# A graph network on one core: in the last pass the own rows are added by products and the sums copied by ScalarE; in the first attention the own rows are weighted by VectorE

## The reference, cut to what matters

```python
e = a_src[src] + a_dst[dst]                 # per edge and head, then leaky relu
e_exp = jnp.exp(e - segment_max(e, dst)[dst])
alpha = e_exp / segment_sum(e_exp, dst)[dst]
out = segment_sum(h[src] * alpha[:, :, None], dst).reshape(N, 256) + bias
out = relu(out)
out = out / maximum(sqrt(sum(out * out, -1)), 1e-12)
x = layernorm(x + out)
```

## Time and profile before

| | us |
|---|---|
| median of three runs | 6150.03 |
| lowest, highest | 6143.17, 6152.39 |
| the profiled execution | 6138.69 |
| its span, first to last instruction | 6136.9 |

### The profile page before, as it was taken

How to read it: one execution, slowest core, us unless ns; L and a number is a source line. 1 busy time by engine, 2 the same in 40 slices (tenths; PEclk the granted TensorE clock), 3 DMA queues, 4 the chain that set the end, 5 groups by cost and what they waited for, 6 DMA issues and landing times. The chain is left out here.

```text
span 6136.9 us, 94789 instructions
## 1 busy us (share of the span) xinstructions
PE 5167.8 (84%) x23690; PEld 3888.2 (63%) x23690; DVE 4560.9 (74%) x13038; ACT 3817.9 (62%) x11901; POOL 3041.7 (50%) x2581
## 2 busy tenths in 40 slices
PE   2788899999999988888888998988899989945654
PEld 1566666666677776767666666667777767733443
DVE  7676655555677787887787888878878777768886
ACT  0587765666899766666655555565555567755555
POOL 1677777422444455555355665543333230057776
PEclk7899999999999999999988888889999989955555
DMA  1577543343566554545344444434544431134442
GB/s 49 183 266 255 193 136 113 125 142 112 195 221 220 184 183 165 190 171 183 137 141 155 157 154 159 161 109 141 166 153 152 137 109 54 39 115 138 139 138 94
DMA packets 362734, 925.74 MB, mean 151 GB/s; under 512 B 66872, under 2 KB 140715, under 8 KB 362198
## 3 DMA queue, kind: packets, MB, share of 16 engines
q1 hardware_dynamic: 271078, 702.73, 33.4%
q0 software_dynamic: 91120, 216.96, 12.1%
HBM read 568.39 MB, written 361.72 MB: 152 GB/s over the span
## 5 line engine op out<-in xcount | busy, mean ns | idle before, releaser
L2207 POOL DMA_INDIRECT got<-hop,end_i x600 | 642.6, 1071 | 725.0 <-PE psum L1014 466.0
L2207 POOL DMA_INDIRECT got<-tab,end_i x600 | 702.8, 1171 | 441.7 <-PE psum L1122 266.7
L1122 PE MATMUL psum<-got,sf 128*128 128x264 f32 (+2 forms) x1200 | 470.4, 482 | 365.0 <-DVE got L1946 288.4
L1014 PE MATMUL psum<-got,sf 128*128 128x256 f32 x1600 | 507.1, 399 | 104.8 <-ACT got L1278 96.8
L1122 PEld LDWEIGHTS psum<-got,sf 128*128 128x128 f32 x1200 | 238.8, 240 | 470.6 <-DVE got L1946 350.4
L1014 PEld LDWEIGHTS psum<-got,sf 128*128 128x128 f32 x1600 | 289.5, 195 | 269.4 <-issue 99.8
L2298 POOL DMA_INDIRECT out<-res,out_i x200 | 211.4, 1057 | 463.9 <-DMA out<-hd 358.0
L963 PE MATMUL psum<-h_t,w 128*128 128x512 f32 x784 | 380.3, 616 | 68.5 <-DVE h_t L1705 68.5
L1162 ACT ACTIVATE squares<-res,l_sv 128x256 f32<-128x256 f32 x600 | 297.3, 496 | 223.7 <-DVE l_sv L1851 188.7
L1278 ACT COPY got<-psum 1x256 f32<-1x256 f32 x796 | 280.0, 352 | 239.2 <-PE psum L1014 184.2
L1316 ACT ACTIVATE res<-res,l_mo 128x256 f32<-128x256 f32 x600 | 310.8, 589 | 147.7 <-DVE l_mo L1839 147.5
(11 more groups left out here) (438 smaller groups left out, 14914.2 us busy)
## 6 DMA issues: line engine op xcount, KB each, us to landing
own<-hop SPq DMA_DIRECT2D x150, 512.0 KB
x_t<-res SPq DMA_DIRECT2D x150, 512.0 KB
xo<-x_t SPq DMA_DIRECT2D x150, 512.0 KB, 3.7
hop<-res SPq DMA_DIRECT2D x100, 512.0 KB
x_in<-in_x SPq DMA_DIRECT2D x98, 512.0 KB, 4.6
out<-hd SPq DMA_DIRECT2D x98, 512.0 KB
tab<-tab SPq DMA_DIRECT2D x50, 536.0 KB, 2.7
own<-tab SPq DMA_DIRECT2D x50, 536.0 KB
```

The source lines that it names most:

```text
L1014: T.matmul(o, sf_of(q)[:, k * P:(k + 1) * P], got_of(q)[:, k * FEAT:(k + 1) * FEAT], start=(p < 3), stop=True).then_inc(at("l_agg"), 1)
L1122: T.matmul(bank(3 + k % 2)[:, 0:g.ext], sf_[:, k * P:(k + 1) * P], got_of(q)[:, k * g.width:k * g.width + g.ext], start=True, stop=True).t ...
L2207: eng.indirect_dma_start(out=dst, out_offset=None, in_=table, in_offset=bass.IndirectOffsetOnAxis(ap=idx, axis=0), bounds_check=rows_ - 1, ...
```

## The change

In the planner: pass 4's `mine` moves from GpSimd to DVE, and the lengths of `vals`, `mine`, `merge`, `u`, `sqr` and `agg` are changed; pass 6 gets ACT parts `ev0` to `ev3` and loses `rlu`. On PE, `agg` k of pass 6 becomes two products into one bank, `ident0` by the own rows and the selection matrix by the linked rows; both stand behind the wait for `g_v`. From k = 2 on they also wait for ACT's copy out of that bank. On DVE, `agg` k of pass 6 keeps only the carry row. On ACT, `ev` k waits for the DVE read of that bank and copies it with relu onto the own rows (the relu of the sum is the same before the division, whose divisor is positive). `merge` waits for the four copies. The sum per row for the shift, before an output of `rlu`, is now an accumulator output of `u`, after which DVE waits for it and scales it.

```diff
--- before.py
+++ after.py
@@ -408,22 +408,27 @@
                 put(("T", "spr", q), 1.8 if p == HOPS else 1.0, here("Vmax", "Sselm"), bank="ring", emptied=here("Vspr"))
                 put(("V", "spr", q), 0.75, here("Tspr", "Vmax") + early("S", "exp"))
                 put(("S", "exp", q), 0.3, here("Vspr") + early("V", "merge"))
-                put(("V", "vals", q), 2.0 if p == HOPS else 0.8, here("Sexp", "Ggather"))
-                me = "Gmine" if p == HOPS else "Vmine"
-                put((me[0], "mine", q), 3.1 if p == HOPS else 0.75, here("Sexp", "Yown"))
+                put(("V", "vals", q), {4: 1.45, 5: 0.8, 6: 1.45}[p], here("Sexp", "Ggather"))
+                put(("V", "mine", q), {4: 1.45, 5: 0.75, 6: 1.3}[p], here("Sexp", "Yown"))
                 put(("V", "lead", q), 0.45, here("Vvals") + early("V", "agg3", 1))
                 for k in range(K):
                     bank_ = [("V", f"agg{k - 2}", q)] if k >= 2 else [("V", f"agg{k + 2}", q - 1)] if j else [("V", "x1a0", q - 1), ("V", "x1a1", q - 1)]
-                    put(("T", f"agg{k}", q), 0.6, here("Vlead" if k == 0 else f"Vagg{k - 1}", "Ssel") + bank_)
-                    put(("V", f"agg{k}", q), 0.78 if p != 5 else 0.5, here(f"Tagg{k}", me))
+                    if p == 6:
+                        if j > 2 * ng or k >= 2:
+                            bank_ = [("S", f"ev{k - 2}", q) if k >= 2 else ("S", f"ev{k + 2}", q - 1)]
+                        put(("T", f"agg{k}", q), 1.05, here("Vlead" if k == 0 else f"Vagg{k - 1}", "Ssel", "Vmine") + bank_)
+                        put(("V", f"agg{k}", q), 0.45, here(f"Tagg{k}"))
+                        put(("S", f"ev{k}", q), 0.42, here(f"Vagg{k}"))
+                    else:
+                        put(("T", f"agg{k}", q), 0.6, here("Vlead" if k == 0 else f"Vagg{k - 1}", "Ssel") + bank_)
+                        put(("V", f"agg{k}", q), 0.78 if p != 5 else 0.5, here(f"Tagg{k}", "Vmine"))
                 free_ = room if p != 5 else ([("T", "tz", q - 2)] if i >= 2 else [])
-                put(("V", "merge", q), {4: 3.2, 5: 1.0, 6: 1.7}[p], here("Vagg3") + ([("S", "sqv", q - 2)] if p == 4 else []) + free_ + (here("Yxo") if p == 4 else []) + early("V", "merge", 1))
+                put(("V", "merge", q), {4: 2.7, 5: 1.0, 6: 1.7}[p], here("Vagg3") + (here("Sev3") if p == 6 else []) + ([("S", "sqv", q - 2)] if p == 4 else []) + free_ + (here("Yxo") if p == 4 else []) + early("V", "merge", 1))
             if p == 6:
-                put(("S", "rlu", q), 1.75, here("Vmerge") + [("V", "u", q - 2)] * (i >= 2))
-                put(("S", "sqr", q), 1.75, here("Srlu") + [("V", "sn", q - 2)] * (i >= 2))
+                put(("S", "sqr", q), 2.4, here("Vmerge") + [("V", "sn", q - 2)] * (i >= 2))
                 put(("V", "sn", q), 0.2, here("Ssqr") + [("V", "u", q - 2)] * (i >= 2))
                 put(("G", "rn", q), 1.05, here("Vsn"))
-                put(("V", "u", q), 1.8, here("Grn", "Yxo") + [("S", "sqv", q - 2)] * (i >= 2))
+                put(("V", "u", q), 2.3, here("Grn", "Yxo") + [("S", "sqv", q - 2)] * (i >= 2))
                 put(("S", "sqv", q), 2.1, here("Vu") + [("V", "sv", q - 2)] * (i >= 2))
                 put(("V", "sv", q), 0.2, here("Ssqv") + [("V", "sh", q - 2)] * (i >= 2))
                 put(("G", "rs", q), 1.05, here("Vsv") + [("S", "norm", q - 2)] * (i >= 2))
@@ -1115,12 +1120,18 @@
             elif name[:3] == "agg":
                 k = h
                 eng.wait_ge(at("g_v"), K * j + k + 1)
-                if K * j + k >= 2:
+                if K * j + k >= 2 * ng * K + 2:
+                    eng.wait_ge(at("g_ev"), K * i + k - 1)
+                elif K * j + k >= 2:
                     eng.wait_ge(at("g_num"), K * j + k - 1)
                 else:
                     eng.wait_ge(at("l_x1a"), 2 * ng)
-                T.matmul(bank(3 + k % 2)[:, 0:g.ext], sf_[:, k * P:(k + 1) * P], got_of(q)[:, k * g.width:k * g.width + g.ext],
-                         start=True, stop=True).then_inc(at("l_agg"), 1)
+                o = bank(3 + k % 2)[:, 0:g.ext]
+                if p == 6:
+
+                    eng.wait_ge(at("g_w"), j + 1)
+                    T.matmul(o, ident0[:], by_chunk(own_of(q), g.width)[:, k, 0:g.ext], start=True, stop=False)
+                T.matmul(o, sf_[:, k * P:(k + 1) * P], got_of(q)[:, k * g.width:k * g.width + g.ext], start=(p < 6), stop=True).then_inc(at("l_agg"), 1)
             elif name == "tz":
                 eng.wait_ge(at("g_o"), j + 1)
                 turn_rows(eng, name, q, 0, z[:, par, 0:K * P].rearrange("p (k f) -> p k f", k=K))
@@ -1359,15 +1370,17 @@
                 for k in range(K):
                     m = S.activation(rec[:, par, k * FEAT:(k + 1) * FEAT], res_of(q)[:, k, :], ACT.Square, scale=1.0 / 16, accum_out=l_ss[:, par, 0, k:k + 1])
                 m.then_inc(at("g_sq"), 1)
-            elif name == "rlu":
+            elif name[:2] == "ev":
+
+                k, w = int(name[2]), layers[6].ext
+
+                if k < K - 1:
+                    eng.wait_ge(at("g_v"), K * (q - HOPS * ng) + k + 2)
+                else:
+                    eng.wait_ge(at("g_cr"), q - HOPS * ng + 1)
+                S.activation(by_chunk(own_of(q), layers[6].width)[:, k, 0:w], bank(3 + k % 2)[:, 0:w], ACT.Relu).then_inc(at("g_ev"), 1)
+            elif name == "sqr":
                 eng.wait_ge(at("g_o"), q - HOPS * ng + 1)
-                if i >= 2:
-                    eng.wait_ge(at("g_u"), i - 1)
-                for k in range(K):
-                    m = S.activation(res_of(q)[:, k, :], res_of(q)[:, k, :], ACT.Relu, accum_out=l_sv[:, par, 0, k:k + 1])
-                m.then_inc(at("g_relu"), 1)
-            elif name == "sqr":
-                eng.wait_ge(at("g_relu"), i + 1)
                 eng.wait_ge(at("g_sq"), ng)
                 eng.wait_ge(at("g_ss"), ng)
                 if i >= 2:
@@ -2069,6 +2082,12 @@
                 if g.loops > 1:
                     V.tensor_scalar(pp[:, par, 1, 0:hk], pp[:, par, 1, 0:hk], float(g.loops), None, ALU.mult).then_inc(at("g_lp"), 1)
                 V.tensor_tensor(got_e, got_e, by(pp[:, par, 0, 0:hk]).unsqueeze(3).to_broadcast([P, K, g.heads, g.cols + 1]), ALU.mult).then_inc(at("g_vv"), 1)
+            elif name == "mine" and p == HOPS:
+                eng.wait_ge(at("g_p"), j + 1)
+                eng.wait_ge(*own_landed(q))
+                c4, weight = split_heads(own_f, g), by(pp[:, par, 1, 0:hk])
+                V.tensor_tensor(c4, c4, weight.unsqueeze(3).to_broadcast([P, K, g.heads, g.cols]), ALU.mult)
+                V.tensor_copy(own_f[:, :, g.flat:g.ext], weight).then_inc(at("g_w"), 1)
             elif name == "mine":
                 eng.wait_ge(at("g_p"), j + 1)
                 if g.loops > 1:
@@ -2090,10 +2109,15 @@
                     if j >= 2:
                         eng.wait_ge(at("g_v"), K * (j - 1) + 1)
                     V.tensor_copy(carry[:, par, 0:g.ext], row).then_inc(at("g_cr"), 1)
+                if p == 6:
+                    return
                 eng.wait_ge(at("g_w"), j + 1)
                 V.tensor_tensor(own_f[:, k, 0:g.ext], bank(3 + k % 2)[:, 0:g.ext], own_f[:, k, 0:g.ext], ALU.add).then_inc(at("g_num"), 1)
             elif name == "merge":
-                eng.wait_ge(at("g_num"), K * (j + 1))
+                if p == 6:
+                    eng.wait_ge(at("g_ev"), K * (i + 1))
+                else:
+                    eng.wait_ge(at("g_num"), K * (j + 1))
 
                 sums, total = (split_heads(own_f, g), own_f[:, :, g.flat:g.ext]) if p == HOPS else (own_e[:, :, :, 0:g.cols], own_e[:, :, :, g.cols])
                 V.tensor_scalar(by(den[:, par, 0, 0:hk]), total, 1e-16 if p == 5 else 0.0, 1e-3, ALU.add, ALU.max).then_inc(at("g_da"), 1)
@@ -2109,8 +2133,8 @@
                 else:
                     room_in_res(eng, q)
                     o = res_of(q).rearrange("p k (h c) -> p k h c", h=g.heads)
-                m = V.tensor_tensor(o, sums, by(den[:, par, 1, 0:hk]).unsqueeze(3).to_broadcast([P, K, g.heads, g.cols]), ALU.mult)
-                m.then_inc(at("g_o"), 1)
+                inverse = by(den[:, par, 1, 0:hk]).unsqueeze(3).to_broadcast([P, K, g.heads, g.cols])
+                V.tensor_tensor(o, sums, inverse, ALU.mult).then_inc(at("g_o"), 1)
                 eng.wait_ge(at("g_o"), j + 1)
                 if p == HOPS:
                     eng.wait_ge(*xo_landed(q))
@@ -2135,11 +2159,13 @@
                 eng.wait_ge(*xo_landed(q))
                 if i >= 2:
                     eng.wait_ge(at("d_sq"), sq_done["sqv", q - 2][1])
-
-                V.scalar_tensor_tensor(l_sv[:, par, 1, :], l_sv[:, par, 0, :], -1.0 / (16 * FEAT), l_ss[:, par, 2, :], ALU.mult, ALU.mult)
                 for k in range(K):
-                    m = V.scalar_tensor_tensor(res_of(q)[:, k, :], res_of(q)[:, k, :], l_ss[:, par, 2, k:k + 1], xo_of(q)[:, k, :], ALU.mult, ALU.add)
-                m.then_inc(at("g_u"), 1)
```

(13 more changed lines are left out.)

## The result

The changed kernel takes 6245.76 us (median of 4, 6239.57 to 6246.82), the kernel before in the same comparison 6147.73 (6143.17 to 6152.39): ratio 1.0157, 95% interval 1.0140 to 1.0175, so 98 us slower. The forecast was 27 us slower, with a range that ended at 6232. The profiled execution has a span of 6237.8 us (before 6136.9).

The account below looks back on a forecast made before the run. No engine is full; DVE and PE hand the carry row to and fro. Per group -1.2 + 2.0 - 0.3 = +0.5 us, 48 groups +24, first attention +3: +27, 6177 us against the median, range 6108 to 6232.

Parts of the forecast that it names:

- The sign: Whole kernel: the change makes it slower, +27 us; chance of slower by over 0.2% put at 0.49.
- step (4): Last pass, PE: own product queued behind the `g_v` wait lengthens each step by 0.87 us, 2.1 in place of 1.23.
- rival D: Last pass: nearly all of 3.5 us paid and ACT's copies late, +1.9 us per group, 6240 us; chance 0.49 including main forecast.
- Step (1) with (2): Last pass, DVE: four adds go, -1.4 us; sums per row in `u` add 0.15; some -1.2 us per group.
- Step (3): Last pass, PE: four products of `ident0` by 260 columns add 3.5 us of work per group (bounds 1.8 and 4.9).
- Step (5): Last pass: DVE's other work covers part of the delay; 0.5 of 0.8 us per step paid, +2.0 us per group.
- Step (6): Last pass, ACT: four copies replace four `rlu`, work about even; later products' wait for copies put at 0, up to +0.5 us.
- Step (7): Last pass, PE clock: fuller streaming raises the granted clock from 0.51 to 0.55-0.6, giving back some 0.3 us per group.
- The first attention: Fifth pass: `mine` moves to DVE, blocked time beside GpSimd goes, `lead` comes later; +3 us taken, bounds -20 and +25.
- Rival A: Last pass: DVE's other work covers PE's delay and its relief counts; -0.5 to -1 us per group, some 6115 us; chance 0.20.
- Rival B: Last pass: denser PE keeps the upper clock for half the stage; -1.0 us per group or better, some 6100 us; chance 0.12.
- Rival C: Last pass: relief and delay cancel, within 12 us either way, 6150 us; chance 0.19.

Follow-up runs that it names:

- e13: e2 with ScalarE's four copies of the last pass cut from 260 to 4 columns, same order: ratio 1.0017 to the kernel before, last stage 724.4 us.
- e9: Kernel before with DVE's four adds of the last pass cut to 4 of 260 columns, order untouched: ratio 0.9974, last stage 701.4 us.
- e1: Changed kernel with the last pass's wait for `g_v` moved behind the own product: ratio 1.0025 to the kernel before, last stage 746.8 us.
- e3: Last pass's part of the change alone, fifth pass as in the kernel before: ratio 1.0070, last stage 788.1 us.
- e2: Changed kernel without the four own products of the last pass, copies and order kept: ratio 1.0010 to the kernel before, last stage 725.7 us.
- e8: Kernel before with the traced lengths in the planner for the last pass, so only the order differs: ratio 1.0045, last stage 740.3 us.
- e4: First attention's part of the change alone, last pass as in the kernel before: ratio 1.0025, last stage 715.3 us.
- e11: Changed kernel with own product ahead of the wait, traced planner lengths, and each own product issued twice: ratio 1.0024 to the kernel before, last stage 722.9 us.
- e10: e4 with DVE's `mine` of the fifth pass ranked behind `lead`: ratio 1.0027 to the kernel before, last stage 713.4 us.
- e7: Changed kernel with the traced lengths in the planner for the last pass, products where the change has them: ratio 1.0135 to the kernel before, stage 777.9 us.
- e12: Kernel before with two constant products ahead of each wait for the carry row in the last pass: ratio 1.0120, last stage 778.3 us.
- e16: Changed kernel with own product ahead of the wait, traced planner lengths, and `mine` behind `lead`: ratio 1.0002 to the kernel before, last stage 716.5 us.
- e5: The changed kernel run again, unaltered: ratio 1.0137 to the kernel before, last stage 784.6 us.

## Why the prediction was wrong, step by step

The sign was right, and the mechanism of step (4) was there; the size was that of rival D (6240), which I had given the end of my own case, at +1.9 us per group. The stage shows +2.1. That D has the number is luck: it wanted nearly all of 3.5 us paid and late copies on ACT, and the waits for sums grew by 2.3 while the copies cost nothing that e13 can tell.

- **Step (1) with (2), the failed one.** I put the relief of DVE into the sum in full: -1.2 us per group, -58 us over 48 groups. DVE's work did fall by that much, but e9 shows that 1.0 us off DVE gives 0.28 us of the period (0.35 by the whole kernel). My own reading of the rows ("no engine is full") had said why, and then the sum treated DVE as the bound and had no term for its other waits, which grew by 1.35 us per group in the changed kernel (powers and L1118). With a quarter of the relief, my sum is -0.3 + 2.0 - 0.3 = +1.4 us per group, 67 us of the 90.
- **Step (3)** held: two products by 260 columns at the low clock last 1.24 us with the own rows and 1.07 behind them, together 2.1 us. PE's busy time rose by 2.8 us per group, not 3.5.
- **Step (4)** held, and e1 shows it alone: the place of the product costs 41 of the 74 us by which e3 is longer than 714.
- **Step (5)** was about right: DVE's waits for sums grew by 2.3 us per group, forecast 2.0. Of the period, the place of the product costs some 0.9 and its work some 0.5 (e1, e2).
- **Step (6)**: the copies cost nothing that can be told (e13). What I had at zero without a run is the new order of the lists. e8 shows that an order alone can cost 28 us, but of this change's order no run shows the price. If e9's relief were all that is left, e2 should have a stage 13 us under before's; it has 12 us more, so some 24 us would come with the rest of the edit: the order, the longer chain through `u` with its sums, and the merge that waits for ScalarE. By the whole kernel, with e4's part taken off, the same difference is 7 us with an interval of some 18 either way, so it isn't shown to be there at all. What is shown is that the waits for GpSimd's powers come with the rest of the edit: 71.9 us of 600 in e2, 11.4 in e9, which has the relief in the order of before, and 54.9 for L2269 alone in e8.
- **Step (7)**: the clock is 0.54, forecast 0.55 to 0.6. The 0.3 us that it should give back is not borne out: at 0.79 (e11) the period is no shorter.
- **The first attention**: forecast +3 us (bounds -20 and +25), 10 at the start of the last stage; e4's ratio is 0.25% (16 us). The pass grew by 3.2%, where I had said within 2%, and DVE's multiply stayed at 1456 ns where I had 1217. I had written that `lead` comes 0.4 us later, and counted DVE's balance alone; e10 shows that the later `lead` is what made the pass longer.
- **Rival A** needed cover between the steps and then the relief of DVE in full. e7 has the cover, with 0.5 us of waiting for sums per group, and its stage is as long; e9 shows that the relief doesn't count in full. **Rival B** fell twice: the clock hardly rose (0.54 for 0.51), and where it was made to rise (e11, e12) the period stayed or grew. **Rival C** is what e16 comes to, with the two edits that this change didn't have.

The split of the last stage, all beside 714: own product's place 41, its work 21, the rest 12. Only the first is confirmed by the whole kernel (46); it has 10 for the work and -10 for the rest, each with an interval that takes in zero. So the place of the product is shown as the largest part, and how the remainder falls on its work, the order and the longer chain is open.

## What to carry to other kernels

A product added to a chain of hand-offs belongs ahead of the wait that it doesn't need: the same work cost 62 us behind it and 21 in front (56 and 10 by the whole kernel). Where no engine is full, don't credit relief of an engine in full; cut its instruction to a few columns in the kernel at hand and see what comes (here 13 of 46 us, and 22 of 60). And where a planner writes the order, a change of its lengths is an edit of its own, worth 28 us here, which has to be run by itself before it is counted as nothing.

## What the runs showed that I had not expected

**The clock without a gain.** The granted clock of the last stage went from 0.59 to 0.79 by products that only repeated others, and the period didn't follow. The Trainium skill ("TensorE: Matmul & The Clock Gate", on the two states) says that sustained activity releases the slow clock; rows of e11 and e12 agree, and show that in a stage of hand-offs the faster level can be without value.

**Two conditions of the chip.** In twelve of the runs every kernel, the one before too, took some 400 us more (6539 to 6590 for 6148 to 6153). The time is in the first passes. Windows of 196 to 1400 us, columns as rows 1, of the kernel before in the first trace and of e4, whose first passes are the same code:

```profile
196.00:1400.00 1204.00, 1096.26 (x4477) 778.50 (x4476) 735.48 (x1936) 828.90 (x2501) 788.96 (x772) 0.97 0.55 181
```

```profile
196.00:1400.00 1204.00, 853.73 (x3118) 590.73 (x3119) 561.61 (x1555) 630.03 (x1953) 676.77 (x657) 0.84 0.44 144
```

The transfers move 144 GB/s in place of 181, and PE gets through 3118 instructions in that time, not 4477. e5 has the first row's picture (181 GB/s). Later passes differ little (714 for 697.5 us in the last stage). It isn't a matter of two chips: under one chip number the kernel before took 6589.56 us beside e1 to e4 and 6152.96 beside e5 to e8, some 20 minutes later. What makes this difference was not found. It hits the kernel before and the changed one alike in the first passes, and the ratios compare kernels within one condition.
